# A recurrence kernel whose first, last and closing stages are rewritten: constants and loads set apart, last segment without lists for a next one, closing block in another order

## The chip, the cores and the metric

One core of a Trainium2 chip runs one program. The metric is the device time of that program in microseconds (us), the median of several executions. The engines are PE (TensorE), DVE (VectorE), ACT (ScalarE), POOL (GpSimd) and SP (SyncE, which only issues DMAs here). PEld is TensorE's weight load.

## The reference

The program computes four layers in a row: a gated delta-rule attention, a small mixture of experts, a softmax attention and a second mixture of experts, each with a residual and a layer norm. The change touches the first alone. Input x is (2, 1024, 128), with 8 heads, keys of 64 and values of 128 channels:

```
q, k, v = silu(conv4(x @ Wq.T)), silu(conv4(x @ Wk.T)) * 64**-0.5, silu(conv4(x @ Wv.T))
a    = sigmoid(x @ Wa.T + ba)          # decay, one number per value channel
beta = sigmoid(x @ Wb.T + bb)          # one number per head
for t in range(T):                     # S is (batch, head, 64, 128), from zero
    err = k_t @ S - v_t
    S   = a_t * S - beta_t * outer(k_t, err)
    o_t = q_t @ S
o = (o - mean) * rsqrt(var + 1e-5) * ln_w + ln_b
return (o * sigmoid(x @ Wg.T)) @ Wo.T
```

## The kernel before, in words

`delta_attention` is four blocks. A block ends when every engine has come to its end and met the others at a barrier, so it lasts as long as its slowest engine or load.

**First block (L176 to L213).** SP issues all loads: Wq, Wk, Wv into `wraw`, four copies of the convolution taps into `wtap` (1 MB each), small ones, `wo`, the input `xT`, `wa`, `wg`, `conv_b`, `ln_w`, `ln_b` and the residual `x_tok`. It waits for the last eight of them. DVE clears `state`, `kq` and `mt` (L201 to L203), multiplies weights and taps in four operations (L207) and scales small tensors and `wo` (L213). POOL builds the constants (`make_constants`, L76 to L127): the identity, a centring matrix, the head masks that the recurrence multiplies with, and masks that only later layers use.

**Second block (L634 to L686).** It prepares segment 0 (64 time steps of both batches): PE makes the projections with their convolution (L345), ACT their activations, POOL products of neighbouring keys (`near`, L538), then 16 copies of keys and queries into `kq` (L552), then scaled values (L527). DVE computes decays and their prefix products (`scan`, L560) and the inverses of small triangular blocks (L482 to L504), and last applies the head masks to the first products (`dve_masks`, L582).

**The recurrence (L696 to L920).** There are 16 segments of 4 chunks of 16 steps, two batches, so 8 "halves" in a segment. A half starts chunk `cc` of batch `x` and ends the previous chunk of the other batch `y`. Inside a chunk four sub-blocks are solved one after another: DVE multiplies and reduces (`solve`, L873 and L876), PE transposes the result (`turn`, L726), ACT copies it (`keep`, L830), PE takes its share off the rest (`take_off`, L737). Then `finish` (L743, L750) and DVE's `update` of the state (L889) let `start` (L708, L715) begin the next chunk of that batch. Every engine's order is written out by hand. Between these steps stand the items of a ring of three PSUM banks, from a list with four slots for each half:

```python
BOTH = [["k0.0"], ["k0.1"], ["k1.0"], ["k1.1", "p0"],
        ["q0.0"], ["q0.1"], ["b", "a0"], ["n", "a1", "p1"],
        ["wo.0"], ["wo.1"], ["a2"], ["a3", "p2"],
        ["g0.0"], ["g0.1"], ["c0"], ["p3"],
        ["g1.0"], ["g1.1"], ["c1"], ["p4"],
        ["var", "q1.0"], ["q1.1"], ["v0.0"], ["v0.1", "p5"],
        ["v1.0"], ["v1.1"], ["v2.0"], ["v2.1", "p6"],
        ["v3.0"], ["v3.1"], ["dt"], ["p7"]]
```

`k`, `q`, `v`, `a`, `b`, `n` and `dt` prepare the next segment, `p` are key products for the coming chunk, and `wo`, `g`, `c` and `var` finish the outputs of the segment before (projection with `wo`, gate, centred values, variance). The last segment runs the same list, so it prepares a segment that is not used. DVE's parts of this work are cut into pieces as well (`dve_piece`, L419).

**Closing block (L922 to L950).** It finishes the outputs of segment 14 first (normalised, gated, projected, L426 to L437), then makes gate, centred values and variance of segment 15. Its reciprocal standard deviation is spread to all partitions by way of DRAM and POOL (L613 to L619, L567, L568), then come normalising, gating and projecting again.

## Time and profile before

| | us |
|---|---|
| median of 3 runs (1963.08 to 1965.64) | 1964.63 |
| the profiled execution, its own time | 1965.2 |
| its span in the trace | 1963.5 |
| first block, to 32.6 | 32.6 |
| second block, 32.6 to 79.5 | 46.9 |
| recurrence, segments 0 to 14, to 999.6 | 920.1 |
| recurrence, segment 15, to 1060.7, and its last steps to 1069.3 | 69.7 |
| closing block, to 1101.8 | 32.5 |
| the other three layers | 861.7 |
| first block: POOL's last constant ends; the last load, `x_tok`, lands | 32.1; 27.2 |
| second block: DVE's chain without a pause, from L484 to L582 | 53.9 to 77.2 |
| segment 15, fourth and fifth half, from `start` to `start` | 6.3; 6.9 |
| closing block: the deviations have landed, L426 begins | 1092.9 |

Over the span PE is busy 87%, DVE 72%, ACT 51% and POOL 31%. The stages follow each other with a barrier between, so a stage's share of the time is read from that stage alone.

### The profile page before, as it was taken

The numbers are of one execution on the slowest core, as the hardware profiler recorded it, in microseconds if no ns is written. First come the engines' busy times: TensorE is split into PE (matmuls) and PEld (weight loads), VectorE is DVE, ScalarE is ACT, GpSimd is POOL, SyncE is SP. The second block draws the span as 40 slices with busy tenths as digits, with TensorE's granted clock in tenths as the row PEclk, the third lists the DMA queues.
The fourth block names the chain that finished last, engine by engine and source line by source line (L and its number), as shares of the span: only waits on it lengthen the run. The fifth ranks groups of instructions, "written<-read, shape, count | busy, mean of one in ns | idle before, by whom it ended". The sixth has DMA issues, their size and how long they took to land. (4 is left out here: it accounts for less than half of the span.)

```text
span 1963.5 us, 42737 instructions
## 1 busy us (share of the span) xinstructions
PE 1717.9 (87%) x15860; PEld 1464.6 (75%) x15860; DVE 1410.0 (72%) x3247; ACT 998.0 (51%) x2633; POOL 611.8 (31%) x986
## 2 busy tenths in 40 slices
PE   3599999899999999999997299799999999998795
PEld 2488788787878778778786266588888888888795
DVE  4687777877778777787776477566666666664777
ACT  1356555455555555556553222555666665653353
POOL 6254345443455434554344000000000000001653
PEclk9799999999999999999998699899999999999898
DMA  4123331223313333222330200890000000003232
GB/s 187 52 73 69 74 81 47 68 69 76 75 46 72 73 74 66 56 72 72 75 73 24 87 1 0 138 58 1 2 2 1 2 1 2 1 2 103 66 89 75
DMA packets 151328, 108.18 MB, mean 55 GB/s; under 512 B 34220, under 2 KB 139384, under 8 KB 150232
## 3 DMA queue, kind: packets, MB, share of 16 engines
q1 hardware_dynamic: 148632, 100.36, 23.3%
q0 software_dynamic: 2496, 5.13, 0.8%
q8 instruction: 127, 2.08, 0.5%
q14 instruction: 73, 0.60, 0.1%
HBM read 87.37 MB, written 18.09 MB: 54 GB/s over the span
## 5 line engine op out<-in xcount | busy, mean ns | idle before, releaser
L577 POOL TENSOR_TENSOR kfull<-kt,pair_rows 128x512 f32<-128x512 f32 x128 | 143.7, 1122 | 514.3 <-ACT kt L365 504.4
L345 PE MATMUL ps<-xT,taps 128*128 128x128 f32 x2176 | 294.0, 278 | 0.1
L345 PEld LDWEIGHTS ps<-xT,taps 128*128 128x128 f32 x2176 | 274.8, 196 | 8.0 <-issue 7.6
L830 ACT COPY wt<-ps 32x128 f32<-32x128 f32 x512 | 131.2, 256 | 260.8 <-PE ps L726 253.8
L1560 DVE TENSOR_REDUCE b_nmax<-ps 128x1 f32<-128x128 f32 (+7 forms) x256 | 180.6, 752 | 72.9 <-PE ps L1397 72.9
L873 DVE TENSOR_TENSOR prod<-ps,mt 128x128 f32<-128x128 f32 x512 | 147.4, 288 | 74.6 <-PE ps L737 59.0
L726 PE MATMUL ps<-ident,w 128*128 128x128 f32 x512 | 162.5, 317 | 34.1 <-ACT wt L830 19.7
L1537 POOL COPY b_spread<-b_inv 128x256 f32<-128x256 f32 x64 | 25.6, 401 | 513.0 <-DVE b_inv L1563 513.0
L876 DVE TENSOR_REDUCE w<-prod 128x32 f32<-128x128 f32 x512 | 146.6, 286 | 17.5
L726 PEld LDWEIGHTS ps<-ident,w 128*128 128x128 f32 x512 | 87.9, 172 | 84.6 <-DVE w L876 73.6
L1489 ACT ACTIVATE b_prob_long<-ps,b_nmax 128x1024 f32<-128x1024 f32 (+3 forms) x128 | 121.3, 952 | 55.8 <-DVE b_nmax L1560 55.8
L1397 PE MATMUL ps<-b_kT,b_qT 64*128 64x256 f32 (+1 forms) x1280 | 142.2, 366 | 0.0
L1429 PEld LDWEIGHTS ps<-b_probT,b_v 128*64 128x64 f32 x2304 | 124.5, 137 | 21.6 <-issue 20.8
L1429 PE MATMUL ps<-b_probT,b_v 128*64 128x128 f32 x2304 | 139.9, 276 | 0.6 <-ACT b_probT L1516 0.6
L737 PE MATMUL ps<-gq,wt 128*128 128x32 f32 x768 | 126.7, 247 | 11.3 <-ACT wt L830 10.1
L750 PE MATMUL ps<-wt,kfull 128*128 128x128 f32 x1024 | 136.2, 277 | 0.0
L737 PEld LDWEIGHTS ps<-gq,wt 128*128 128x128 f32 x768 | 116.7, 192 | 23.5 <-ACT wt L830 20.6
L560 POOL TENSOR_TENSOR di<-di 128x128 f32<-128x128 f32 x240 | 126.8, 528 | 17.6
L1570 DVE COPY b_probT<-ps 128x512 f32<-128x512 f32 (+1 forms) x192 | 115.4, 621 | 17.1 <-PE ps L1409 14.4
L1489 ACT ACTIVATE b_prob_short<-ps,b_nmax 128x128 f32<-128x128 f32 (+3 forms) x128 | 66.3, 522 | 118.0 <-DVE b_nmax L1560 118.0
L750 PEld LDWEIGHTS ps<-wt,kfull 128*128 128x128 f32 x1024 | 125.5, 193 | 0.0
L1397 PEld LDWEIGHTS ps<-b_kT,b_qT 64*128 64x128 f32 x1280 | 108.1, 187 | 13.8
(281 smaller groups left out, 3888.7 us busy)
## 6 DMA issues: line engine op xcount, KB each, us to landing
decay<-ends_dram SPq DMA_DIRECT2D x256, 128.0 KB, 5.8
gn<-near_dram SPq DMA_DIRECT2D x34, 384.0 KB, 6.6
slots_dram<-zero SPq DMA_DIRECT2D x1, 9216.0 KB, 58.8
rr<-rates_dram SPq DMA_DIRECT2D x34, 256.0 KB, 4.4
sq<-rstd_dram SPq DMA_DIRECT2D x17, 512.0 KB, 3.6
wtap<-in_taps SPq DMA_DIRECT2D x4, 1024.0 KB, 11.3
f_w<-in_f_w SPq DMA_DIRECT2D x2, 2048.0 KB, 11.0
s_xb<-slots_dram SPq DMA_DIRECT2D x46, 64.5 KB, 1.9
```

Of the source, the lines that this page charges most:

```text
L345: mm = pe.matmul(part, lhsT=taps[:, tap, t * P:(t + 1) * P], rhs=xT[:, :, columns(at_next) - LOOK + tap:columns(at_next) - LOOK + tap + TS ...
L577: nc.gpsimd.tensor_tensor(kfull[:, n % 4, :, :], kt[:, n % 2, :].unsqueeze(1).to_broadcast([P, G, P]), cst["pair_rows"][:, :].unsqueeze(2) ...
L726: pe.transpose(ps[:, 2, 0:P], w[:, b, :, :, :].rearrange("p i h s -> p (i h s)"), cst["ident"][:, :]).then_inc(wt_ready[b], 1)
L737: pe.matmul(ps[:, b, cols], lhsT=wt[:, b, :], rhs=gq[:, n % 4, 0, cols], start=False, stop=True, skip_group_check=True).then_inc(z_ready[b ...
L750: mm = pe.matmul(ps[:, 4 + b, g * P:(g + 1) * P], lhsT=kfull[:, n % 4, g, :], rhs=wt[:, b, :], start=False, stop=True, skip_group_check=True)
L830: nc.scalar.copy(wt[rows, b, :], ps[rows, 2, 0:P]).then_inc(wt_kept[b], 1)
L873: ch.step(nc.vector.tensor_tensor(prod[:, b, :, :, :], zi, mtc[:, :, b, NB * c + i, :, :], ALU.mult))
L876: nc.vector.tensor_reduce(w[:, b, i, :, :], prod[:, b, :, :, :], axis=AX.X, op=ALU.add).then_inc(w_ready[b], 1)
L1397: mm = pe.matmul(scores_of(w, long, h)[:, c0:c1], lhsT=qT[rows, f, b * T + i * P:b * T + (i + 1) * P], rhs=kT[rows, f, b * T + c0:b * T + ...
L1429: pe.matmul(ps[cols, 7, long * P:(long + 1) * P], lhsT=v[:, f, b * TT + j, cols], rhs=probT[:, at_probT(w, long, h * n + j), :], start=(j ...
L1489: nc.scalar.activation(prob[long][:, h, 0:tiles(w, long) * P], scores_of(w, long, h), ACT.Exp, bias=nmax[:, w % 2, j:j + 1], accum_out=tot ...
L1560: nc.vector.tensor_reduce(nmax[:, w % 2, j:j + 1], scores_of(w, j // 2, j % 2), axis=AX.X, op=ALU.max, negate=True).then_inc(max_done, 1)
```

## The change

- `make_constants` keeps what the first block and PE's first work need. The rest becomes `make_masks`, which POOL runs in the second block, between `near` and the 16 copies; DVE waits for it (`masks_made`) only before its last step there.
- The fill of `mt` with zeros moves from DVE to POOL in the first block.
- Loads of `wo`, `wg` and `x_tok` go to the end of SP's order. The first block waits for none of them: DVE waits for `wo` at the head of the second block and scales it there, SP waits for `wg` and `x_tok` at that block's end.
- In segment 15 the lists hold only `wo`, `g`, `c`, `var` and `p0` to `p6`; the DVE, ACT, POOL and SP work for a next segment is left out there as well.
- The closing block is written anew. PE takes the centred values of segment 15 first, then the gate, then the variance; segment 14's outputs are finished while the standard deviation of segment 15 travels. Segment 15 has buffers of its own (`cs_last`, `sq_last`, `gate_last`, in the room of `taps`).

```diff
-    def __init__(self, slots, by_vector):
+    def __init__(self, slots, by_vector, ending=None):
+        self.slots, self.by_vector, self.ending = slots, by_vector, ending or slots
...
+    def slots_of(self, f):
+        return self.ending if f == NS - 1 else self.slots
...
-    ch.step(nc.gpsimd.memset(cst["mean_col"][:, :], 1.0 / P))
...
+def make_masks(nc, ch, cst):
+    select = nc.gpsimd.affine_select
     ch.step(nc.gpsimd.memset(cst["head_masks"][:, :, :], -1.0 / DK))
...
-                                     (bias_b[:, 0:1], d["bb"]), (wo[:, :, :], d["WoT"])):
+                                     (bias_b[:, 0:1], d["bb"])):
                         sp.dma_start(dst, src).then_inc(load_b, 16)
...
-                    for dst, src in ((wa[:, :], d["WaT"]), (wg[:, :], d["WgT"]), (conv_b[:, :], d["conv_b"]),
-                                     (ln_w[:, :], d["ln_w"]), (ln_b[:, :], d["ln_b"]), (res[:, 1:, :], d["x_tok"])):
+                    for dst, src in ((wa[:, :], d["WaT"]), (conv_b[:, :], d["conv_b"]),
+                                     (ln_w[:, :], d["ln_w"]), (ln_b[:, :], d["ln_b"])):
                         sp.dma_start(dst, src).then_inc(load_w, 16)
-                    sp.wait_ge(load_w, 16 * 8)
+                    sp.dma_start(wo[:, :, :], d["WoT"]).then_inc(load_wo, 16)
+                    for dst, src in ((wg[:, :], d["WgT"]), (res[:, 1:, :], d["x_tok"])):
+                        sp.dma_start(dst, src).then_inc(load_late, 16)
+                    sp.wait_ge(load_w, 16 * 6)
...
                     make_constants(nc, pool, cst_made, cst)
+                    nc.gpsimd.memset(mt[:, :, :, :, :], 0.0)
...
-                    nc.vector.memset(mt[:, :, :, :, :], 0.0)
...
-        both = Ring(BOTH, BY_DVE)
+        both = Ring(BOTH, BY_DVE, [[x for x in part if x.split(".")[0] in POST + PRODUCTS[:-1]] for part in BOTH])
...
+                sp.wait_ge(load_late, 16 * 2)
...
                 pool_prepare(pool, only_pre, 0, 0, "near")
+                make_masks(nc, Chain(pool, S["masks_chain"]), cst)
+                nc.gpsimd.memset(cst["mean_col"][:, :], 1.0 / P).then_inc(S["masks_made"], 1)
                 pool_prepare(pool, only_pre, 0, 0, 0)
...
+                dve.wait_ge(load_wo, 16)
+                nc.vector.tensor_scalar(wo[:, :, :], wo[:, :, :], 0.5, None, ALU.mult)
...
                 dve.wait_ge(z_ready[0], 1)
+                dve.wait_ge(S["masks_made"], 1)
                 dve_masks(0, first_products, w_ready[0])
...
-                    if c == 1:
+                    if c == 1 and f < NS - 1:
                         sp_spread_rates(sp, both, f, 1 - f % 2)
...
-                    if j == 5:
+                    if j == 5 and f < NS - 1:
                         scan(ch, nc.gpsimd.tensor_tensor, f, nx)
...
+        cs_last, sq_last, gate_last = (taps[:, k, 0:H * N] for k in range(3))
...
+                for k in range(2):
+                    pe.matmul(ps[:, k, :], lhsT=cst["centre"][:, :], rhs=of[:, k * HALF:(k + 1) * HALF], start=True,
+                              stop=True).then_inc(E["centred"], 1)
...
+                pe.wait_ge(E["squared"], 2)
...
+                mm.then_inc(E["var_done"], 1)
+                out(0, cs)
+                out(1, cs_last)
...
+                    act.wait_ge(E["centred"], k + 1)
+                    nc.scalar.activation(sq_last[:, part], ps[:, k, :], ACT.Square).then_inc(E["squared"], 1)
+                    nc.scalar.copy(cs_last[:, part], ps[:, k, :])
+                act.wait_ge(E["var_done"], 1)
+                nc.scalar.copy(var_rows[:, :], ps[:, 4, 0:PART]).then_inc(E["var_kept"], 1)
+                norm(0, cs[:, :])
...
+                scale(cs, sq)
+                gating(0, cs, gate)
+                add(0)
+                dve.wait_ge(S["rstd_in"], 16)
+                scale(cs_last, sq_last)
+                dve.wait_ge(E["gate_kept"], 2)
+                gating(1, cs_last, gate_last)
+                add(1)
```

How the instructions stand now. **POOL, second block.** The engine's order before, from `near` to the scaled values:

```order
L538 TENSOR_TENSOR near<-qk 128x128
L552 COPY kq<-qk 64x8x4x4 [waits a_near_done,a_ring_act]
L552 COPY kq<-qk 64x8x4x4 x7
L552 COPY kq<-qk 64x8x4x4 [waits a_near_done,a_ring_act,a_copied]
L552 COPY kq<-qk 64x8x4x4 x7
L527 TENSOR_TENSOR vd<-vd,di 128x32x15 [waits a_d_done,a_ring_act,a_copied]
```

and of the change the place where the masks come in (L113, L115 and L122 are the selects that were L98, L100 and L107), with the engine's end of them:

```order
L554 TENSOR_TENSOR near<-qk 128x128
L108 MEMSET head_masks 128x256
L113 AFFINE_SELECT head_masks<-head_masks 32x128 [waits a_masks_chain]
L115 AFFINE_SELECT head_masks<-head_masks 32x128 [waits a_masks_chain]
L118 MEMSET head_masks 32x32 [waits a_masks_chain]
...
L140 MEMSET ident 128x128 [waits a_masks_chain]
L141 AFFINE_SELECT ident<-ident 128x128 [waits a_masks_chain]
L689 MEMSET mean_col 128x1 [waits a_masks_chain]
L568 COPY kq<-qk 64x8x4x4 [waits a_near_done,a_ring_act]
L568 COPY kq<-qk 64x8x4x4 x7
```

Between `near` and the copies there are now 31 selects and 13 fills.

**PE, segment 15, the half with j = 6.** Before, from `start` to the end of the half:

```order
L715 MATMUL ps<-kq,state 64x8x8 x7
L726 MATMUL ps<-ident,w 128x128 [waits a_wt_kept1,a_w_ready1]
L345 MATMUL ps<-xT,taps 128x128 [waits a_ring_act]
L345 MATMUL ps<-xT,taps 128x128 x3
L737 MATMUL ps<-gq,wt 128x32 [waits a_wt_kept1]
L726 MATMUL ps<-ident,w 128x128 [waits a_wt_kept1,a_w_ready0]
L345 MATMUL ps<-xT,taps 128x128 x4
L737 MATMUL ps<-gq,wt 128x32 [waits a_ring_dve,a_wt_kept0]
L726 MATMUL ps<-ident,w 128x128 [waits a_wt_kept0,a_w_ready1]
```

and of the change the same stretch (L748 is `turn`, L759 `take_off`):

```order
L737 MATMUL ps<-kq,state 64x8x8 x7
L748 MATMUL ps<-ident,w 128x128 [waits a_wt_kept1,a_w_ready1]
L759 MATMUL ps<-gq,wt 128x32 [waits a_wt_kept1]
L748 MATMUL ps<-ident,w 128x128 [waits a_wt_kept1,a_w_ready0]
L759 MATMUL ps<-gq,wt 128x32 [waits a_ring_dve,a_wt_kept0]
L748 MATMUL ps<-ident,w 128x128 [waits a_wt_kept0,a_w_ready1]
```

The convolutions between the steps of the two chains are gone; what stands in the row now waits for ACT or DVE at each instruction.

**PE, closing block.** Before:

```order
L316 MATMUL ps<-wo,cs 128x128 [waits a_gated]
L316 MATMUL ps<-wo,cs 128x128 x3
L324 MATMUL ps<-xT,wg 128x128 x8
L328 MATMUL ps<-vd,centre 128x512 [waits a_ring_dve]
L328 MATMUL ps<-vd,centre 128x512 [waits a_ring_act]
L304 MATMUL ps<-sq,mean_rows 32x256 [waits a_ring_act]
```

and of the change:

```order
L961 MATMUL ps<-vd,centre 128x512 x2
L965 MATMUL ps<-xT,wg 128x128 x8
L971 MATMUL ps<-taps,mean_rows 32x256 [waits a_end_squared]
L971 MATMUL ps<-taps,mean_rows 32x256 x3
L955 MATMUL ps<-wo,cs 128x128 [waits a_end_gated]
```

The projection of segment 14 stood ahead of centring and variance, and stands behind them now.

## Rows read from the trace of the kernel before

**Rows 1.** Busy time by stage: window, length, each engine's busy time, PEclk, DMA share, GB/s
```profile
0.00:32.60 32.60, 0.00 (x0) 0.00 (x0) 21.20 (x11) 0.00 (x0) 27.94 (x60) 1.00 0.72 274
32.60:79.50 46.90, 24.22 (x162) 20.16 (x162) 24.96 (x45) 16.04 (x41) 15.16 (x28) 0.79 0.11 31
999.60:1060.70 61.10, 56.16 (x527) 48.63 (x527) 48.48 (x123) 33.65 (x96) 28.40 (x46) 1.00 0.34 68
1069.30:1101.80 32.50, 11.40 (x60) 9.46 (x60) 5.75 (x10) 6.11 (x9) 1.90 (x2) 0.63 0.05 17
```

**Rows 2.** Timeline of the first block, POOL and DVE: start, length, engine, line, operation
```profile
7.94 6.88 DVE L203 MEMSET mt<- 128x8192 f32 x1 [1.66 <-issue]
10.81 6.26 POOL L107 TENSOR_SCALAR_AFFINE_SELECT head_masks<-head_masks 32x32 f32<-32x32 f32 x1
...
17.14 2.44 POOL L98 TENSOR_SCALAR_AFFINE_SELECT head_masks<-head_masks 32x128 f32<-32x128 f32 x1
...
26.36 0.55 POOL L98 TENSOR_SCALAR_AFFINE_SELECT head_masks<-head_masks 32x128 f32<-32x128 f32 x1
```

**Rows 3.** Loads of the first block: tile wtap, SP's timeline, and time to landing
```profile
L207 DVE TENSOR_TENSOR taps<-wraw,wtap x4: 2228/2374/2459, 14.7 to 21.5; 128x2048 f32<-128x2048 f32 x4
DMA to landing us min/median/max: 8.3/11.3/14.4
2.19 2.31 SPq L182 DMA_DIRECT2D wtap<-in_taps  x4
14.91 0.45 SPq L190 DMA_DIRECT2D ln_b<-in_ln_b  x1
ln_b<-in_ln_b SPq DMA_DIRECT2D x1, 0.5 KB, 10.3
```

**Rows 4.** Timeline of the second block, POOL and DVE
```profile
34.02 0.95 POOL L667 MEMSET cs<- 128x1024 f32 x1
...
41.96 1.78 POOL L538 TENSOR_TENSOR near<-qk 128x384 f32<-128x384 f32 x3 [5.20 <-ACT qk L405]
...
51.85 5.42 POOL L552 COPY kq<-qk 64x128 f32<-64x128 f32 x16 [8.11 <-ACT qk L403]
...
66.34 1.49 DVE L492 TENSOR_TENSOR tmp<-gn,mt 128x256 f32<-128x256 f32 x1
...
72.33 0.62 DVE L492 TENSOR_TENSOR tmp<-gn,mt 128x256 f32<-128x256 f32 x1
```

**Rows 5.** Timeline of segment 15 and of its last steps, the solve chain
```profile
1004.73 0.30 PE L726 MATMUL ps<-ident,w 128*128 128x128 f32 x1
...
1005.09 1.06 PE L750 MATMUL ps<-wt,kfull 128*128 128x128 f32 x8
...
1006.19 0.69 DVE L889 TENSOR_TENSOR state<-ps,decay 128x512 f32<-128x512 f32 x1 [0.60 <-PE ps L750]
...
1029.79 0.69 DVE L889 TENSOR_TENSOR state<-ps,decay 128x512 f32<-128x512 f32 x1
...
1031.26 0.29 DVE L873 TENSOR_TENSOR prod<-ps,mt 128x128 f32<-128x128 f32 x1
...
1061.65 0.28 DVE L873 TENSOR_TENSOR prod<-ps,mt 128x128 f32<-128x128 f32 x1
...
1062.31 0.33 PE L726 MATMUL ps<-ident,w 128*128 128x128 f32 x1 [2.11 <-DVE w L876]
...
1063.65 0.29 DVE L873 TENSOR_TENSOR prod<-ps,mt 128x128 f32<-128x128 f32 x1 [1.40 <-PE ps L737]
```

**Rows 6.** Busy time in a stretch at the end of the recurrence, columns as in rows 1
```profile
1059.00:1062.00 3.00, 1.20 (x9) 0.83 (x8) 2.93 (x6) 0.76 (x2) 0.80 (x1) 1.00 0.00 0
```

**Rows 7.** Timeline of the closing block
```profile
1076.67 1.95 PE L324 MATMUL ps<-xT,wg 128*128 128x128 f32 x16
...
1078.46 1.88 PE L328 MATMUL ps<-vd,centre 128*128 128x512 f32 x4
...
1082.43 0.37 ACT L372 COPY var_rows<-ps 128x256 f32<-128x256 f32 x1 [0.84 <-PE ps L304]
```

More of the change, by code:

```diff
@@ L855, in _ @@
                         act_norm(act, both, f)
-                    if j in (3, 4):
+                    if j in (3, 4) and f < NS - 1:
                         act_diagonal(act, f, 1 - f % 2, j - 3)
@@ L925, in _, with out @@
             def _(pe):
-                for item in only_post.names:
-                    pe_item(pe, only_post, 0, 1, item, 0, NS - 1)
-                for item in only_post.slots[0]:
-                    pe_item(pe, only_post, 1, 1, item, 0, NS - 1)
+                def out(k, values):
+                    pe.wait_ge(E["gated"], 2 * k + 2)
+                    for h in range(H):
+                        mm = pe.matmul(ps[:, 6 + k, 0:C], lhsT=values[:, h * N:(h + 1) * N], rhs=wo[:, h, :], start=(h == 0),
+                                       stop=(h == H - 1))
+                    mm.then_inc(E["out_done"], 1)
@@ L931, in _ @@
+                pe.wait_ge(E["squared"], 2)
+                for u in range(4):
+                    mm = pe.matmul(ps[32 * u:32 * u + 32, 4, 0:PART], lhsT=cst["mean_rows"][:, :],
+                                   rhs=sq_last[:, u * PART:(u + 1) * PART], start=True, stop=True, skip_group_check=True)
+                mm.then_inc(E["var_done"], 1)
+                out(0, cs)
+                out(1, cs_last)
             @block.scalar
             def _(act):
-                act_norm(act, only_post, 0)
@@ L934, in _, with norm @@
-                for item in only_post.order:
-                    act_item(act, only_post, 0, 1, item)
-                act_norm(act, only_post, 1)
+                def norm(k, values):
+                    act.wait_ge(E["scaled"], 2 * k + 2)
+                    nc.scalar.activation(values, values, ACT.Identity, bias=ln_b[:, 0:1], scale=ln_w[:, 0:1]).then_inc(
+                        E["normed"], 1)
+                for k in range(2):
+                    part = slice(k * HALF, (k + 1) * HALF)
+                    act.wait_ge(E["centred"], k + 1)
+                    nc.scalar.activation(sq_last[:, part], ps[:, k, :], ACT.Square).then_inc(E["squared"], 1)
+                    nc.scalar.copy(cs_last[:, part], ps[:, k, :])
@@ L938, in _ @@
+                act.wait_ge(E["var_done"], 1)
+                nc.scalar.copy(var_rows[:, :], ps[:, 4, 0:PART]).then_inc(E["var_kept"], 1)
+                norm(0, cs[:, :])
+                for k in range(2):
+                    act.wait_ge(E["gate_done"], k + 1)
+                    nc.scalar.activation(gate_last[:, k * HALF:(k + 1) * HALF], ps[:, 2 + k, :], ACT.Tanh, scale=0.5).then_inc(
+                        E["gate_kept"], 1)
+                norm(1, cs_last)
             @block.gpsimd
@@ L953, in delta_attention, with scale, gating @@
-        stage_end(nc, every)
+                def scale(values, factors):
+                    for k in range(2):
+                        part = slice(k * HALF, (k + 1) * HALF)
+                        nc.vector.tensor_tensor(values[:, part], values[:, part], factors[:, part], ALU.mult).then_inc(
+                            E["scaled"], 1)
+                def gating(n, values, gates):
+                    dve.wait_ge(E["normed"], n + 1)
+                    for k in range(2):
+                        part = slice(k * HALF, (k + 1) * HALF)
+                        stt(out=values[:, part], in0=gates[:, part], scalar=1.0, in1=values[:, part], op0=ALU.add,
+                            op1=ALU.mult).then_inc(E["gated"], 1)
@@ L956, in layer_norm @@
+                add(1)
+        stage_end(nc, every + list(E.values()))
 def layer_norm(nc, ctx, cst, ps, res, xT, name, loads=(), arrived=(), out=None):
```

66 lines of the change are left out of this document (45 added, 21 removed).

## The prediction

> **What bounds the kernel now.** I read the table of windows by stage first, since barriers part the stages, and then the timeline of each stage that the change touches, asking what ends last there.
>
> The first block lasts 32.6 us. DVE is busy for 21.2 of them, POOL for 27.9 [rows 1]. POOL ends last: its list of constants reaches to 32.1, and the last load to be waited for lands before 28. That list is stretched by DVE. A select takes 0.55 us alone, 2.44 beside DVE's products of weights and taps, and a smaller one took 6.26 [rows 2].
>
> The second block, 46.9 us, has no busy engine [rows 1]. DVE's chain ends it: from 53.9 to 77.2 it stands still nowhere, while POOL waits.
>
> Segment 15 takes 61.1 us with PE busy for 56.2 [rows 1]. PE is the bound there, and much of its work prepares a segment that does not exist.
>
> The closing block takes 32.5 us with PE busy for 11.4 [rows 1]: one serial path, in which the variance of segment 15 is copied out only at 1082.4 [rows 7], 13.1 us in; the way from there to the block's end, DMAs by DRAM and then norm, gate and projection, is 19.4.
>
> **First block.** Removed from POOL: 31 selects and 13 small fills. Added: the fill of `mt`, 8192 elements. A fill of 1024 takes 0.95 us there [rows 4], so 8 x 0.95 = 7.6, from 3.4 to 11. DVE loses its own fill, 6.88 us [rows 2], and is free at 6.3. Its four products, 2.2 to 2.5 us each, began at 14.7 behind that fill. The taps land 8.3 to 14.4 us after issues that begin at 2.2 and end at 4.5 [rows 3], so from 10.5 to about 18; the last product then ends at 20.3, the small scalings at 20.7. The loads decide: `ln_b`, issued at 14.91, landed 10.3 later, at 25.2 [rows 3]. Two loads of 512 KB, `wo` and `wg`, now stand behind it. Three MB of taps land within 7.5 us (10.5 to 18), so 512 KB are 1.25 us: `ln_b` lands at 22.7. Before, the next block began 0.5 us behind POOL's end, so now it begins at 23.1 in place of 32.6: **-9.5**. Bounds: -6.9 if `ln_b` lands no earlier (25.2 + 0.5), -11.4 if DVE were the last (20.7 + 0.5).
>
> `wo` lands about 1.3 us after `ln_b`. DVE waits for it at the head of the second block and scales it in some 0.7 us, and has nothing to do until 15 us into that block: 0. `x_tok` lands by 28, while SP's first own DMA of the block comes 11 us in: 0. Without that cover each would cost its own time.
>
> **Second block.** `near` ends at 43.7 [rows 4], 11.1 us into the block. The masks come next: 16 large selects at 0.61 with the gap, 15 small ones at about 0.3, 13 fills at about 0.2 make 17 us. Alone they would end 28 us in; the copies (5.4 us for 16 [rows 4], begun 19 us in before) then end at 34. PE's first products were held until 33.4 by DVE's scan, and DVE took them only 44 us in: covered by 10 us. The price lies elsewhere: while masks and copies last, DVE's chain meets POOL. DVE's four products, with no gap between, took 2.23 us at the least and 2.46 at the most [rows 3], the longest ones those with a large select just ahead: 0.23 for 0.55 of POOL. The three POOL operations per DVE operation that I count let about 18 selects (4 large, 14 small) fall beside DVE's chain: 4 x 0.23 + 14 x 0.06 = 1.7, and the copies, nine more than now beside it, 0.5: **+2.2**. Bounds: 0 where DVE finds the gaps, and the whole POOL operation each time: 4 x 0.55 + 14 x 0.2 + 9 x 0.34 = 8.1. For the upper end speaks L492, 1.49 us beside a POOL product of two inputs and 0.62 without one [rows 4]; I stay near the lower value since these are selects and copies, of one input, as in the row of 2.46.
>
> The Trainium skill (SBUF — State Buffer, "SBUF: two separate sides") calls the port that DVE and GpSimd share "an exclusive lock, not a bandwidth split", held for the whole instruction. It speaks against this part of the change. By it the term would be the upper end, some 8 us; the trace agrees for L492 and shows less than half of it for the selects.
>
> **Segment 15.** Gone from PE are 16 tiles of convolution, `a`, `b`, `n`, `dt` and `p7`, from DVE the decays and inverses, from POOL `scan`, copies and scaled values. What is left is bounded by the chain of the two batches, so I add one half up from update to update. From L889 to the solve of the other batch, 1.47 (1029.79 to 1031.26); once around solve, turn, keep, take off, 2.00 (1061.65 to 1063.65); solve to turn 0.66 (to 1062.31); turn to L750 0.36 (1004.73 to 1005.09); L750 to L889 1.10 [rows 5]. The sum is 5.6. PE's own row (product of keys, then `start`) makes `start` 0.1 late: 5.7, times 8 is 45.6. On top: scaling, and ACT's norm of 1.24 us ahead of a `keep`, 0.5 in the first half and 1.2 in the second; the projection between the steps of the third, 0.8; gate and centring in the fourth and fifth, 0.5 together. That makes 48.6, and 61.1 - 48.6 = **-12.5**. Bounds: halves four and five, which carry only `g` and `c` already, take 6.3 and 6.9 now; eight of 6.6 would be 52.8, so -8.3. The path without any delay, 44.8, and half of the additions, 1.5, give -14.8. What is late next is DVE's solve, not a DMA: the decay rows for chunk 63 are asked for three chunks ahead.
>
> **Closing block.** PE begins with centring (1.88 us), gate (1.95) [rows 7] and variance (0.64). These rows were taken at 2.4 GHz. In this block the granted clock is 0.63 on average [rows 1]: it stood at 1.2 GHz from the recurrence's end through PE's idle start, and rose to 2.4 in the course of the first projection. With about 4 us of it at 1.2 GHz, the 4.5 us of work become 6.5, and the copy of the variance begins 6.7 us in, not 13.1: **-6.4**. Bounds: full clock 4.7 in (-8.4), 1.2 GHz throughout 9.2 in (-3.9). The outputs of segment 14 take 1.29 + 1.24 + 1.29 + 3.6 + 0.3 and lie inside the 10.5 us until the deviations land: 0. The way from the copy to the end keeps its 19.4.
>
> **Sum.** -9.5 + 2.2 - 12.5 - 6.4 = -26.2. From the profiled execution's 1965.2 that gives 1939.0. The median of the runs lies 0.6 below that execution, so I say **1938.5**. About 0.2% (3.9 us) can be told from no change.
>
> **Rivals.**
> - *The port is a full lock.* The second block pays 8.1 in place of 2.2, and the total is 1944.4. For it: L492, and the select of 2.44. Against: 2.46 beside 2.23. The page named above states this mechanism. Chance 0.16.
> - *The late loads do not get out of the way,* so the first block doesn't do what it says. All loads share the same DMA engines; if the small ones behind `wa` land at 25.2 as before, the first block gives 6.9: 1941.1. For it: SP's issues were held up at `ln_w`. Against: loads landed in the order of issue. Chance 0.12.
> - *The clock falls inside segment 15.* After a stretch in which PE was busy for 1.2 of 3 us [rows 6] the clock fell to 1.2 GHz. There it stays at full speed as long as convolutions fill the gaps. In the new halves PE works for some 3.5 of 5.7 us. If it fell, L750's 1.06 [rows 5] and the other passes would put 1.5 on each half, and projection and gate 1 more: 61, no gain, 1951. Against: PE still has work in every part of a half. Chance 0.08.
> - *Slower: POOL starves.* In the first block a select waited for a whole DVE operation, 2.4 us. If each of the 31 waited like that in the second block, masks would take 31 x 2.4 = 74, the block would end about 90 us in and not at 47: +43 on -28.4, hence 1979.5. It turns slower than before from 1.9 us a select on. Against: DVE's operations there are 0.4 to 0.8 us long. Chance 0.02.
>
> **How the numbers follow.** The forecast has 0.62: the likeliest, so 1938.5. Its own bounds run from 1931 (all gains near their ends) to 1945. The range 1932 to 1947 takes in the first two rivals and leaves out the clock (0.08), starving (0.02) and about 0.08 of tails. Faster by over 0.2%: all but starving and a heap of mishaps, 0.97; within it 0.01; slower 0.02.
>
> **What would show it.** The second block should begin near 23 with SP's load the last to be waited for and POOL idle from 11. Masks should stand between 11 and 32 us into the block, selects up to 1.1 us long, and DVE's chain end 2 us later than the 77.2 - 32.6 of now; if its operations beside selects last 0.5 us longer each, it is the lock. Segment 15's halves should be 5.6 to 6.9 us from L889 to L889, at PEclk 1.00. In the closing block the variance copy should begin 6 to 7 us in. I am wrong if a block's end is held by something I gave no price, if the halves stay above 6.3, or if the clock reads 0.50 within the segment.

## The result and the profile after

The change takes 1940.31 us, the median of 4 runs (1936.63 to 1940.86), against 1964.33 (1963.08 to 1965.64) for the kernel before. The ratio is 0.9874, with a 95% interval from 0.9857 to 0.9891, so the kernel is faster by some 24 us. The profiled execution took 1940.86 us, its span 1938.9. All times below are of executions in the chip's fast state; one in a slow state, of 4190.78 us in the run with the masks made twice, is left out.

By stage, from barrier to barrier (the second column is the length of the stage in the trace of before):

| stage | before | after | difference | forecast |
|---|---|---|---|---|
| first block | 32.6 | 23.15 | -9.5 | -9.5 |
| second block | 46.9 | 46.55 | -0.4 | +2.2 |
| segments 0 to 14 | 920.1 | 921.2 | +1.1 | 0 |
| segment 15 with the last steps | 69.7 | 60.9 | -8.8 | -12.5 |
| closing block | 32.5 | 25.3 | -7.2 | -6.4 |
| the other three layers | 861.7 | 861.75 | 0 | 0 |
| span | 1963.5 | 1938.9 | -24.6 | -26.2 |

Of the 1.1 us in segments 0 to 14, 1.0 lies in the very first half (9.1 us from `start` to `start`, 8.15 before). The traces show the clock there too: its second eight passes of convolution take 1.91 us (L361 at 73.54) and took 1.06 (L345 at 83.32), and the half reads 0.69 where it read 0.78.

A trace is one execution, and a stage that no edit touches differs between traces. In the nine traces below whose kernels leave the first block as in the change it lasts 22.3 to 22.9 us, and in the nine that leave the second block so, that one lasts 45.7 to 47.4.

These are the windows of after: three stages, segment 15 with its last steps, and under the dots its eight halves, from `start` to `start`, the last with the last steps. The columns are those of [rows 1]: length, then busy time of PE, PEld, DVE, ACT and POOL, PEclk, DMA share, GB/s.

```profile
0.00:23.15 23.15, 0.00 (x0) 0.00 (x0) 13.75 (x9) 0.00 (x1) 8.94 (x18) 1.00 0.90 344
23.15:69.70 46.55, 25.38 (x162) 21.06 (x163) 26.94 (x46) 16.14 (x41) 36.19 (x72) 0.77 0.19 52
990.91:1051.85 60.94, 49.01 (x384) 40.33 (x384) 33.81 (x102) 19.65 (x58) 10.42 (x10) 0.83 0.21 44
1051.85:1077.15 25.30, 12.22 (x60) 9.23 (x60) 5.75 (x10) 5.87 (x9) 1.91 (x2) 0.67 0.06 22
...
990.91:999.49 8.58, 6.80 (x42) 5.53 (x42) 5.95 (x17) 1.25 (x5) 1.28 (x1) 0.66 0.49 115
999.49:1007.70 8.21, 6.25 (x43) 5.29 (x42) 4.39 (x12) 2.95 (x7) 1.04 (x1) 0.73 0.27 73
1007.70:1013.93 6.23, 5.67 (x59) 5.19 (x58) 3.55 (x12) 1.79 (x6) 1.04 (x1) 1.00 0.31 42
1013.93:1019.67 5.74, 5.74 (x53) 4.72 (x52) 3.53 (x12) 3.47 (x9) 1.04 (x1) 1.00 0.37 44
1019.67:1025.41 5.74, 5.74 (x53) 4.72 (x52) 3.52 (x12) 3.47 (x9) 1.04 (x1) 1.00 0.02 5
1025.41:1031.23 5.82, 4.92 (x52) 3.71 (x51) 3.54 (x12) 2.16 (x7) 1.04 (x1) 1.00 0.02 3
1031.23:1038.37 7.14, 5.89 (x43) 5.01 (x42) 3.84 (x13) 1.78 (x6) 2.90 (x3) 0.76 0.02 3
1038.37:1051.85 13.48, 8.02 (x55) 6.16 (x53) 5.47 (x18) 2.78 (x9) 1.04 (x1) 0.74 0.13 40
```

Read the PEclk column first. Before it stood at 1.00 over the whole segment [rows 1]. Now the halves 3 to 6 read 1.00 and last 5.7 to 6.2 us, and the halves 1, 2 and 7 read 0.66, 0.73 and 0.76 and last 8.6, 8.2 and 7.1. That is where the missing part of the forecast is. The timeline of PE shows what it is made of, the product of the state (L750 before [rows 5]) in half 1 and in half 3:

```profile
996.28 1.91 PE L772 MATMUL ps<-wt,kfull 128*128 128x128 f32 x8
...
1012.27 1.06 PE L772 MATMUL ps<-wt,kfull 128*128 128x128 f32 x8
```

The same eight passes take 1.91 us at 1.2 GHz and 1.06 at 2.4. The fall itself comes in half 1, and this stretch stands at the lower level throughout:

```profile
993.60:1000.30 6.70, 5.84 (x27) 4.81 (x27) 3.60 (x11) 1.34 (x5) 0.23 (x1) 0.50 0.67 166
```

The first block of after, POOL and DVE, and below it the landing of `ln_b` (median us from issue; it was issued at 10.79):

```profile
3.30 6.93 POOL L217 MEMSET mt<- 128x8192 f32 x1
...
18.19 2.29 DVE L226 TENSOR_TENSOR taps<-wraw,wtap 128x2048 f32<-128x2048 f32 x1 [0.27 <-DMA wtap<-in_taps]
...
23.15 0.96 POOL L681 MEMSET vd<- 128x1024 f32 x1 [12.92 <-POOLq L192]
...
ln_b<-in_ln_b SPq DMA_DIRECT2D x1, 0.5 KB, 12.0
```

POOL ends at 10.2 and stands idle for 12.9 us; DVE ends at 20.7; `ln_b` lands at 22.8 and the next block begins at 23.15. POOL's list, which ended the block at 32.1, has gone from the path, and a load has taken its place.

The second block, POOL and DVE:

```profile
54.76 7.37 POOL L568 COPY kq<-qk 64x128 f32<-64x128 f32 x16
...
62.21 3.00 POOL L543 TENSOR_TENSOR vd<-vd,di 128x480 f32<-128x480 f32 x2
62.64 1.52 DVE L514 TENSOR_TENSOR tmp<-gn,mt 128x256 f32<-128x256 f32 x1
64.20 1.49 DVE L516 TENSOR_TENSOR tmp<-gn,mt 128x256 f32<-128x256 f32 x1
...
66.90 0.41 DVE L598 TENSOR_TENSOR gq<-ps,head_masks 128x256 f32<-128x256 f32 x1
```

The 16 copies stretch from 5.42 [rows 4] to 7.37 us, but DVE's chain, from its first L500 (43.52) to the end of its last L520 (66.99), lasts 23.5 us where it lasted 23.0. The chain is a steadier measure than the block: in the nine other traces it lasts 23.3 to 23.5 us. DVE reaches its last step 4.8 us behind the copies: masks and copies are hidden.

The closing block:

```profile
1051.85 3.54 PE L961 MATMUL ps<-vd,centre 128*128 128x512 f32 x4 [1.66 <-PEq L85]
...
1057.81 0.37 ACT L990 COPY var_rows<-ps 128x256 f32<-128x256 f32 x1 [1.31 <-PE ps L971]
...
1060.70 2.75 PE L955 MATMUL ps<-wo,cs 128*128 128x128 f32 x16 [2.96 <-DVE cs L1026]
...
1072.27 3.59 PE L955 MATMUL ps<-wo,taps 128*128 128x128 f32 x16 [8.82 <-DVE taps L1026]
```

The variance is copied 6.0 us in, not 13.1 [rows 7]. Centring takes 3.54 us where it took 1.88 [rows 7].

### The profile page after: what moved, and what is told of

It reads as the page before. It is cut to its first block and busy times, and to the rows that moved or that the text cites. A ratio compares the mean times of both kernels' runs of the same rounds, so it can differ in the third digit from the quotient of the medians.

```text
span 1938.9 us, 42270 instructions
## 1 busy us (share of the span) xinstructions
PE 1711.4 (88%) x15702; PEld 1455.7 (75%) x15702; DVE 1386.2 (71%) x3217; ACT 984.5 (51%) x2593; POOL 595.3 (31%) x951
## 3 DMA queue, kind: packets, MB, share of 16 engines
q8 instruction: 125, 2.05, 0.5%
## 5 line engine op out<-in xcount | busy, mean ns | idle before, releaser
L361 PE MATMUL ps<-xT,taps 128*128 128x128 f32 x2048 | 278.9, 279 | 0.1
L361 PEld LDWEIGHTS ps<-xT,taps 128*128 128x128 f32 x2048 | 260.6, 197 | 7.6 <-issue 7.2
L748 PE MATMUL ps<-ident,w 128*128 128x128 f32 x512 | 163.0, 318 | 34.7 <-ACT wt L853 18.5
L748 PEld LDWEIGHTS ps<-ident,w 128*128 128x128 f32 x512 | 87.9, 172 | 84.8 <-DVE w L899 73.6
L759 PE MATMUL ps<-gq,wt 128*128 128x32 f32 x768 | 128.3, 249 | 14.2 <-ACT wt L853 13.1
L1518 PEld LDWEIGHTS ps<-b_probT,b_v 128*64 128x64 f32 x2304 | 124.5, 137 | 21.7 <-issue 20.9
L759 PEld LDWEIGHTS ps<-gq,wt 128*128 128x128 f32 x768 | 117.7, 194 | 28.3 <-ACT wt L853 25.3
L576 POOL TENSOR_TENSOR di<-di 128x128 f32<-128x128 f32 x225 | 118.7, 527 | 16.5
## 6 DMA issues: line engine op xcount, KB each, us to landing
f_w<-in_f_w SPq DMA_DIRECT2D x2, 2048.0 KB, 10.7
```

Of the source, the lines that this page charges most:

```text
L361: mm = pe.matmul(part, lhsT=taps[:, tap, t * P:(t + 1) * P], rhs=xT[:, :, columns(at_next) - LOOK + tap:columns(at_next) - LOOK + tap + TS ...
L748: pe.transpose(ps[:, 2, 0:P], w[:, b, :, :, :].rearrange("p i h s -> p (i h s)"), cst["ident"][:, :]).then_inc(wt_ready[b], 1)
L759: pe.matmul(ps[:, b, cols], lhsT=wt[:, b, :], rhs=gq[:, n % 4, 0, cols], start=False, stop=True, skip_group_check=True).then_inc(z_ready[b ...
L1518: pe.matmul(ps[cols, 7, long * P:(long + 1) * P], lhsT=v[:, f, b * TT + j, cols], rhs=probT[:, at_probT(w, long, h * n + j), :], start=(j ...
```

## The experiments

**The parts, one undone at a time.** Four kernels, each the change with one part put back.

Masks to the first block, `mt` to DVE:

```diff
                     make_constants(nc, pool, cst_made, cst)
-                    nc.gpsimd.memset(mt[:, :, :, :, :], 0.0)
+                    make_masks(nc, Chain(pool, masks_chain), cst)
...
-                make_masks(nc, Chain(pool, S["masks_chain"]), cst)
```

> The changed kernel with one part undone: the masks are made by POOL in the first block again, and mt is filled by DVE again; loads, last segment and closing block stay changed. Theory (POOL's list ended the first block, and the masks cost DVE's chain in the second block 0.5 us): first block back to 32.6 us from 23.15, second block 46.0 in place of 46.5, total 1949.4. Rival (the shared port is held for whole instructions, and the second block is as long as it was only because something else got shorter by as much): without masks there the second block falls to 43 or less, total 1946. Rival (the loads end the first block, not POOL): first block stays at 23 to 24, total 1940.

Measured: 1948.85 us (1944.36 to 1953.61). The first block lasts 33.5 us, the second 46.25, and DVE's chain there 22.7. POOL ends the first block again:

```profile
33.09 0.10 POOL L218 MEMSET mean_col<- 128x1 f32 x1
33.49 0.95 POOL L683 MEMSET vd<- 128x1024 f32 x1 [0.30 <-POOLq L192]
```

The theory holds. Without the masks the second block is 0.3 us shorter, less than it differs between traces, and DVE's chain 0.8 (22.7 for 23.5).

Loads in their old order, all waited for in the first block:

```diff
-                                     (bias_b[:, 0:1], d["bb"])):
+                                     (bias_b[:, 0:1], d["bb"]), (wo[:, :, :], d["WoT"])):
...
-                    sp.wait_ge(load_w, 16 * 6)
+                    sp.wait_ge(load_w, 16 * 8)
```

> The changed kernel with one part undone: wo, wg and x_tok stand in the old places of SP's order and the first block waits for all of them; masks stay in the second block. Theory (the last load that is waited for ends the first block, and loads land in the order of issue): the block ends 0.5 us behind x_tok's landing, which was at 27.2 before, so 27.7 in place of 23.15: +4.5, total 1944.8, second block unchanged. Rival (order is of no weight, the small loads land when the taps are through): the block ends at 23 to 24, total 1940 to 1941.

Measured: 1946.67 us (1945.00 to 1947.69), first block 28.15 us (+5.0, forecast +4.5), second 46.7. The block now ends 0.4 us behind the landing of `x_tok` (27.7). So with the masks moved alone the block goes from 32.6 to 28.15 us, with the loads moved alone (the run above) it stays at 33.5; the -9.5 needs both.

Full lists in segment 15:

```diff
-        both = Ring(BOTH, BY_DVE, [[x for x in part if x.split(".")[0] in POST + PRODUCTS[:-1]] for part in BOTH])
+        both = Ring(BOTH, BY_DVE)
...
-                    if j == 5 and f < NS - 1:
+                    if j == 5:
```

> The changed kernel with one part undone: segment 15 runs the full lists for a next segment again, on all engines. Theory (what the short lists gained is the 8.8 us that the traces show, and half clock in three of the halves took the rest of the forecast 12.5): segment 15 with its last steps 69.7 us, granted clock 1.00 through all its halves, the 8 passes of the state product 1.06 us in every half, total 1949.1. Rival (the first two halves are long because of the scaling and normalising of DVE and ACT, not because of the clock): the first two halves are as long as now or longer, 8.6 and 8.2 or more, even though the clock is 1.00, and the total is the same 1949.

Measured: 1948.58 us (1948.36 to 1949.61), segment 15 with its last steps 69.5 us. The windows of its halves 1, 2 and 7:

```profile
991.99:1000.05 8.06, 7.48 (x73) 7.04 (x74) 6.11 (x17) 2.24 (x9) 1.29 (x1) 1.00 0.53 107
1000.05:1009.16 9.11, 8.00 (x77) 6.64 (x76) 4.80 (x13) 7.25 (x21) 2.79 (x4) 1.00 0.08 22
...
1038.14:1046.00 7.86, 7.65 (x75) 7.06 (x74) 6.93 (x16) 2.96 (x12) 7.48 (x17) 1.00 0.11 37
```

PE is busy for 7.5 of 8.1 us and the clock reads 1.00. With short lists it has less to do and the first half is longer, 8.58 us. The term is measured (8.6 us in the trace); whether the clock or DVE's scaling makes the first two halves long, this run can't tell, since PE's own work fills them here.

The old closing block:

```diff
-                def out(k, values):
-                    pe.wait_ge(E["gated"], 2 * k + 2)
...
+                for item in only_post.names:
+                    pe_item(pe, only_post, 0, 1, item, 0, NS - 1)
```

> The changed kernel with one part undone: the closing block in its old order. Theory: variance copied 13 us in and the block 32.5 us again, against 25.3: +7.2, total 1947.5. Rival (the block starts at 1.2 GHz in both orders, so the old order now suffers more, since PE's projection, gate and centring all stand ahead of the variance): variance copied 14 to 16 us in, block 34 to 35, total 1949 to 1950.

Measured: 1944.76 us (1942.56 to 1948.66), 2.7 less than forecast. The block itself costs more than forecast, 33.2 us with the variance copied 13.6 us in (+7.9). The stages that this edit leaves alone are shorter than in the change: the first two by 0.9 us together, segment 15 with its last steps by 1.2, and the three layers behind by 2.0 (859.7). The first 40 us of those layers in two windows of 20, here and below it in the change:

```profile
1082.67:1102.67 20.00, 8.49 (x48) 8.02 (x48) 12.22 (x25) 8.56 (x15) 0.00 (x0) 0.64 0.52 188
1102.67:1122.67 20.00, 12.00 (x46) 7.38 (x47) 14.57 (x32) 3.58 (x6) 0.00 (x0) 0.67 0.00 1
...
1077.15:1097.15 20.00, 9.62 (x44) 9.07 (x45) 11.43 (x24) 8.29 (x14) 0.00 (x0) 0.54 0.48 187
1097.15:1117.15 20.00, 10.87 (x39) 6.96 (x40) 13.06 (x26) 2.67 (x5) 0.00 (x0) 0.60 0.00 0
```

The clock is higher here. That is no price of the new order as such. The change and the runs with masks first, loads first, masks twice and small loads moved read 0.54 or 0.55 and then 0.60, and their last three layers take 861.7 to 862.6 us. The runs with full lists and with unread matmuls in the segment alone have the new order too, read 0.63 to 0.65 and 0.66 to 0.68, and take 859.0 to 859.7. The clock at the head of these layers isn't all of it, since the kernel before reads 0.63 and 0.68 and takes 861.6. So a total moves by 3 us and more with what happens behind the edit.

**Matmuls that nobody reads.** Is it the clock that makes the halves 1, 2 and 7 long? PE gets matmuls of 128x128 into the PSUM bank that the next item will overwrite, two behind each of the first three slots of the halves 1, 2, 7 and 8. They change no result.

```diff
+                def spin(j, k, count):
...
+                    for _ in range(count):
+                        pe.matmul(ps[:, BANKS[(r - 1) % len(BANKS)], 0:P], lhsT=cst["ident"][:, :], rhs=cst["centre"][:, :],
+                                  start=True, stop=True, skip_group_check=True)
...
+                        if f == NS - 1 and j in (0, 1, 6, 7) and k in (0, 1, 2):
+                            spin(j, k, 2)
```

> The changed kernel, and in segment 15 PE gets matmuls that nobody reads: two of 128x128 behind each of the first three slots of the halves 1, 2, 7 and 8 (24 matmuls, some 0.23 us each at full clock, 1.35 us in a half). Theory (the clock fell to 1.2 GHz in these halves because PE had too little to do, and that is why they last 8.6, 8.2 and 7.1 us and not 5.8): granted clock 0.9 to 1.00 there, halves 7.5, 6.6 and 6.0, last steps 0.5 shorter, the closing block's centring 1.9 in place of 3.5; together 4 to 6 us less than the change: 1935 to 1936. Rival (scaling, normalising and the tail of segment 14's vector work make these halves long): halves as long as now plus up to 1.35 us each, total 1940 to 1944.

Measured: 1935.05 us (1931.55 to 1935.89), ratio to the kernel before 0.9844 (0.9830 to 0.9857). Halves 1, 2, 3, 7, and 8 with the last steps:

```profile
989.79:996.52 6.73, 5.80 (x53) 5.03 (x54) 5.34 (x15) 1.24 (x5) 1.29 (x1) 1.00 0.46 107
996.52:1003.26 6.74, 5.64 (x55) 4.89 (x54) 4.64 (x14) 2.95 (x7) 1.04 (x1) 1.00 0.56 129
1003.26:1009.49 6.23, 5.67 (x59) 5.19 (x58) 3.73 (x13) 1.78 (x6) 1.04 (x1) 1.00 0.34 42
1026.80:1032.46 5.66, 5.54 (x55) 4.89 (x54) 3.52 (x12) 1.78 (x6) 2.90 (x3) 1.00 0.02 1
1032.46:1045.60 13.14, 8.80 (x66) 7.27 (x65) 5.71 (x18) 2.78 (x9) 1.04 (x1) 0.78 0.11 41
```

The halves fall from 8.58, 8.21 and 7.14 us to 6.73, 6.74 and 5.66 with more work on PE, and each reads 1.00. That is the clock, and it rules the rival out for what was lost: scaling and normalising are still there. The halves 1 and 2 stay 1.0 us above the 5.74 of halves 4 and 5; how much of that scaling and normalising make was not measured. Segment 15 with its last steps takes 55.8 us, 5.1 less than in the change. In the last steps the clock still falls, and centring begins the closing block at 1.2 GHz as before (3.75 us): that part of the expectation failed. The gate begins at 1.2 GHz as well (2.41 us, 1.95 in the change), so the closing block is 1.2 us longer, 26.5. The three layers behind are 2.7 shorter (859.0).

The dose doubled, `spin(j, k, 4)`:

> As the run before, with four such matmuls in place of two (2.7 us in a half at full clock). Theory: the clock is 1.00 as well, but the matmuls now stand in the way of the two solve chains: halves of 6.5 to 7, total between the dose of two and the change, 1936 to 1939. Rival (no clock effect): 1943 to 1948.

Measured: 1937.22 us (1936.74 to 1937.84). Halves 1, 2 and 7 read 1.00 and last 7.07, 6.90 and 6.34 us. The clock has nothing more to give, and the matmuls stand in the way.

The dose halved, `spin(j, k, 1)`:

> As the run with two unread matmuls a slot, with one (0.7 us in a half at full clock). Theory: what is bought is the clock alone, so if it reads 1.00 with the dose of one, the halves 1 and 2 last 6.4 to 6.7 and the total is that of dose two or up to 0.5 less, 1934 to 1935; if it falls in one of them, that half lasts 8 again and the total is 1936 to 1939. Rival (the unread matmuls help by something other than the clock, such as keeping the queue of PE fed): half of the gain of dose two, halves of 7.6, whatever the clock reads.

Measured: 1934.54 us (1932.62 to 1936.66). The halves 1 and 2 last as long as with dose two:

```profile
991.35:998.08 6.73, 5.33 (x47) 4.37 (x48) 5.35 (x15) 1.23 (x5) 1.29 (x1) 1.00 0.46 108
998.08:1004.82 6.74, 5.08 (x49) 4.22 (x48) 4.64 (x14) 2.95 (x7) 1.04 (x1) 1.00 0.55 128
```

What helps doesn't grow with the dose; it comes with the clock's 1.00. Twelve matmuls in the segment are enough.

**The port that DVE and POOL share.** The masks are made twice in the second block, so that selects stand beside all of DVE's chain.

```diff
-                make_masks(nc, Chain(pool, S["masks_chain"]), cst)
+                masks = Chain(pool, S["masks_chain"])
+                for _ in range(2):
+                    make_masks(nc, masks, cst)
```

> The changed kernel with the masks made twice in the second block, the same instructions once more behind the first, so that POOL's selects stand beside the whole of DVE's chain there (23.4 us long in the change, 22.9 in the kernel before). Theory (a select costs DVE a quarter of a microsecond at most, most find the gaps): DVE's chain 23.5 to 24.5 us. Rival (the port is held for whole instructions): another 16 selects beside the chain cost their own length, the chain lasts 28 us or more. In both cases POOL now ends the block: masks to 76, copies to 82, scaled values and keys to 85; second block 62 us in place of 46.5, total 1955 to 1957.

Measured: 1954.43 us, the median of three (1951.10 to 1956.55), second block 59.2 us. DVE's chain lasts 22.2 us, less than in the change. It must be compared like for like: here POOL's two scaled products come after the chain, while in the other kernels two of DVE's operations meet them and take 1.5 us in place of 0.62 and 0.60. Without that 1.8 the chain of the kernel with no masks there is 22.7 - 1.8 = 20.9. So 32 selects and their fills beside the whole chain cost DVE 1.3 us, where a DVE held off for each whole select would, by estimate, have lost over 10 (17 of them are large selects of 0.54 us, 9.2 us already). One of DVE's operations with a select beginning beside it:

```profile
62.86 0.63 DVE L514 TENSOR_TENSOR tmp<-gn,mt 128x256 f32<-128x256 f32 x1
63.02 0.86 POOL L113 TENSOR_SCALAR_AFFINE_SELECT head_masks<-head_masks 32x128 f32<-32x128 f32 x1
63.52 0.66 DVE L516 TENSOR_TENSOR tmp<-gn,mt 128x256 f32<-128x256 f32 x1
```

It is the select that gets longer (0.86 us, 0.54 alone). The same L514 took 1.52 us beside a POOL product of two inputs, above.

**Small loads.** If `ln_b` ends the first block, move it, and the next one is earlier.

```diff
+                    sp.dma_start(conv_b[:, :], d["conv_b"]).then_inc(load_w, 16)
...
+                    sp.dma_start(wa[:, :], d["WaT"]).then_inc(load_w, 16)
...
-                    for dst, src in ((wg[:, :], d["WgT"]), (res[:, 1:, :], d["x_tok"])):
+                    for dst, src in ((wg[:, :], d["WgT"]), (res[:, 1:, :], d["x_tok"]), (ln_w[:, :], d["ln_w"]),
+                                     (ln_b[:, :], d["ln_b"])):
```

> The changed kernel with three small loads moved: conv_b ahead of xT, ln_w and ln_b behind x_tok among those that the first block doesn't wait for. Theory (the last load that is waited for ends the block, 0.4 us behind its landing): the last is now wa, which landed at 20.7 and may land a little earlier; the block ends at 21.0 to 21.3 (DVE's last scaling ends at 20.7) in place of 23.15; total 1938.3. Rival (SP's own issuing of small loads holds the queue up, and what is moved forward delays the input behind it): block at 22 to 23, total 1939.5 to 1940.5.

Measured: 1941.04 us (1937.67 to 1943.56), first block 22.65 us, within the 22.3 to 22.9 of kernels that move nothing there. No gain: the rival was right. SP's issue of `wa` and of what follows, the landing of `wa`, and the next block's first operation:

```profile
9.14 0.44 SPq L205 DMA_DIRECT2D wa<-in_WaT  x1
9.62 1.21 SPq L206 DMA_DIRECT2D wo<-in_WoT  x1
10.87 2.11 SPq L209 DMA_DIRECT2D wg<-in_WgT  x1
13.02 2.11 SPq L209 DMA_DIRECT2D stream<-in_x_tok  x1
...
wa<-in_WaT SPq DMA_DIRECT2D x1, 512.0 KB, 13.1
...
22.65 0.96 POOL L681 MEMSET vd<- 128x1024 f32 x1 [12.43 <-POOLq L192]
```

`wa` lands at 22.2, 0.4 us ahead of the block's end. It was issued at 7.88 and landed at 20.7 in the change. The last load waited for does end the block; only it comes 1.6 us later itself, being issued 1.3 later.

**A version that beats both.** Matmuls that nobody reads to the end of the layer:

```diff
                 turn(last_chunk, 1, 2)
+                spin(7, 3, 2)
                 take_off(last_chunk, 1, 2)
+                spin(7, 3, 4)
...
+                spin_last(10)
                 out(0, cs)
+                spin_last(24)
                 out(1, cs_last)
```

> The kernel with two unread matmuls a slot, and more of them to the end: between the last steps of the recurrence (16), and in the closing block 10 ahead of segment 14's projection and 24 ahead of the last one, while PE waits there. Theory (half clock costs 0.9 us in the last steps, 2.3 in centring and gate, 1.7 in the last projection): last steps at 1.00, centring 1.9 us, variance copied 4.7 to 5.5 us into the block, last projection 1.9 in place of 3.6; half 8 with last steps 12 in place of 13.1, closing block 23 to 24 in place of 26.5; total 3 to 5 us less than with the dose of two alone, 1930 to 1932. Rival (the barrier's pause is enough for the clock to fall, and matmuls behind it don't bring it back in time): 1934 to 1937, the extra matmuls standing in the way.

Measured: 1932.15 us (1928.55 to 1934.97). The variance is copied 4.4 us into the block, centring takes 1.95. The five times spread over 6.4 us, and the trace is of the second fastest (1928.67). The extra matmuls behind segment 14's projection (x48 are 24 of them, two passes each), and the last projection:

```profile
1054.79 5.52 PE L976 MATMUL ps<-centre,ident 128*128 128x128 f32 x48
1065.47 3.78 PE L970 MATMUL ps<-wo,taps 128*128 128x128 f32 x16 [5.16 <-DVE taps L1048]
```

The 24 matmuls, at full clock, ended 5.2 us too early, and the projection ran at 1.2 GHz: this part of the expectation failed. The closing block takes 24.9 us. The next run changes three things against this one: 42 matmuls in place of the 24, two in place of the eight behind the last step, and no last update of the state, which nobody reads:

```diff
+                    if cc == last_chunk:
+                        return
                     if n >= 1:
                         pe.wait_ge(S["k_kept"], n)
...
-                spin(7, 3, 8)
+                spin(7, 3, 2)
...
-                spin_last(24)
+                spin_last(42)
```

> The kernel with unread matmuls to the end, with three things put right: 42 of them ahead of the last projection in place of 24 (the 24 ended 5.2 us before it, and it lasted 3.8 us at half clock), 2 in place of 8 behind the last step (the 8 ended 1.0 us behind DVE and held the barrier), and the last update of the state, which nobody reads, left out for both batches (the last product of the state with its DVE operation, and the decay rows for it). Theory: the last product and update no longer stand between the last outputs and the barrier, closing block begins 2.3 us sooner (half 8 with last steps 10.7 in place of 12.96); last projection 1.9 to 2.1 at full clock, closing block 23.1 in place of 24.9; total 4 us less than the run before, 1928. Rival (the barrier waits for something else, such as SP's DMAs, or the clock falls in the shorter tail): 1930 to 1932.

Measured: **1929.87 us** (1927.71 to 1930.68), ratio to the kernel before 0.9825 (0.9812 to 0.9839), against 0.9874 (0.9857 to 0.9891) for the change: 10 us faster than the change, by intervals that do not touch. Its gain over the run before, 2.3 us by the medians, is not clear of the spread (1928.55 to 1934.97 there). Half 8 with the last steps, the closing block, and the last projection:

```profile
1033.00:1042.77 9.77, 7.91 (x71) 6.71 (x69) 4.42 (x17) 2.78 (x9) 1.04 (x1) 1.00 0.16 56
1042.77:1065.43 22.66, 20.22 (x164) 18.16 (x164) 5.75 (x10) 5.78 (x9) 1.91 (x2) 1.00 0.08 24
...
1062.09 2.05 PE L975 MATMUL ps<-wo,taps 128*128 128x128 f32 x16 [0.61 <-DVE taps L1053]
```

Both stages are shorter than expected (10.7 and 23.1); the total is 1.9 us above the forecast 1928, since the layers behind take 860.5 us here and took 856.3 in the run before. At their head the clock reads 0.65 and 0.67 here and read 0.59 and 0.74; why they differ by that was not found.

The last update left out of the change, with no extra matmuls:

> The change as it is, with no unread matmuls, and only the last update of the state left out for both batches. Theory (the chain from the last solve to the barrier is shorter by the product, 1.9 at half clock, and the update): last steps 2.5 us shorter, total 1937.5 to 1938. Rival (with yet less work PE's clock stays down for longer, in half 8 and at the head of the closing block): part of it is given back, total 1939 to 1940.

Measured: 1937.93 us (1936.43 to 1940.34). The segment with its last steps takes 57.0 us, 4.0 less than in the change; 3.4 of that lie in half 8 with the last steps (10.06 us at PEclk 0.82, 13.48 at 0.74 before), 0.8 in half 1, in which the clock read 0.86 and not 0.66. No instruction is different up to there, so these 0.8 are the clock's own variation and no gain of the edit. The closing block is 0.8 longer (26.1) and reads 0.63 where the change read 0.67. So the closing block may give something back, as the rival said; the sum is where the theory put it.

## Why the prediction was right, and where not

The median came out at 1940.3 for 1938.5 foretold, inside the range. That it lies so near is partly luck: segment 15 gave 3.7 us less than its term and segments 0 to 14 took 1.1 more, while the second block came out 2.6 below its term and the closing block gave 0.8 more. Of the prediction's own signs of being wrong two came true, halves above 6.3 us (1, 2 and 7) and a clock of 0.50 within the segment. By steps:

- **First block, -9.5: right, and right in what ends the block.** `ln_b` was to land at 22.7 and the next block to begin at 23.1; they did so at 22.8 and 23.15. Undoing either part shows that POOL's list (33.5) and `x_tok` (28.15) had both to go. The rival of late loads that do not get out of the way is ruled out for `ln_b`, which landed at 25.2 before. Why it lands sooner is less sure than the sum has it: the sum counts the megabyte no longer ahead of it, but `ln_b` was also issued 4.1 us sooner (10.79 for 14.91), and with the small loads moved `wa` landed 1.6 us later when issued 1.3 later, with hardly more ahead of it. No run parts the two for `ln_b`. Nor does the first decimal mean much, since other traces of the same block give 22.3 to 22.9 us.
- **Second block, +2.2: mis-sized.** DVE's chain grew by 0.5 us, and the block got 0.4 shorter, since the chain begins 0.9 earlier in it (a difference of the size that untouched blocks show). The price of a select for DVE was taken from one row (0.23 us); the run with masks made twice gives 1.3 us for 32 of them, 0.04 each. The rival, a port held for the whole instruction, priced the term at 8.1 us from rows. The prediction named the rule of the Trainium skill for it (SBUF — State Buffer, "SBUF: two separate sides"), by which whichever of the two engines starts first holds the shared port for its whole instruction. The run with twice the masks speaks against it for selects; L514 and L516, at 1.5 us beside a POOL product of two inputs, agree with it. POOL did not starve either: no select took over 0.95 us.
- **Segment 15, -12.5: the step that failed.** The sum of a half (5.7 us) was right: the undisturbed halves last 5.74. What was wrong is that the term priced every half at 2.4 GHz. Three of eight read 0.66 to 0.76, and the term came to 8.8. The rival "the clock falls inside segment 15" had the mechanism but not the extent: it was priced for all eight halves (no gain), and in the change it struck three that have no projection, gate or centring in PE's list. Which ones is not fixed by the list: with the loads first the halves 1, 2 and 3 read 0.63, 0.70 and 0.87 (8.8, 8.6 and 7.0 us) and half 7 read 1.00 (5.7 us), and half 8 was spared in the change up to the last steps. "PE still has work in every part of a half" did not hold the clock; a single matmul more in a slot does. With the clock held in the halves the segment with its last steps takes 55.8 us, so the term would have been -13.9.
- **Closing block, -6.4: right, 0.8 too small.** The variance was copied 6.0 us in, 6.7 foretold. Centring ran at 1.2 GHz for its length, as assumed, and the clock was up again for the gate (1.95 us).
- **Hidden terms, all at 0:** `wo` is scaled at 23.64 in 1.02 us, and DVE has nothing else to do for 12 us; segment 14's projection ends at 1063.5, 4.8 us before the deviations land. `x_tok` landed at 27.3 and held nothing up. Segments 0 to 14 were put at 0 and took 1.1 more, 1.0 of it in the first half, by the clock.

## What to carry to other kernels

When a change takes filler work from PE and leaves a chain of small dependent steps, price the chain at both clocks, half by half, and read the granted clock before anything else in the new trace. If it reads below 1.00, try a few matmuls that nobody reads before rewriting the order; place them so that the last ends right before the work that counts. Where two things end a block together, here POOL's list and a load behind it, moving one gives only the gap between them. Before a total is read for one stage, compare the stages that the edit leaves alone: here they moved it by 3 us and more.

## What was not expected of the hardware

- The granted clock fell to 1.2 GHz inside a stretch in which PE was busy for 6.8 of 8.6 and 6.3 of 8.2 us by the trace (halves 1 and 2; part of that busy time is itself the slow clock), and read 1.00 with one more 128x128 matmul, some 0.25 us, behind each of three slots in a half.
- The same instructions read differently with what ran before them: the first 40 us of the three layers behind read 0.54 and 0.60 in the change and 0.63 and 0.68 with two unread matmuls a slot in the segment.
- After 5.2 us without work PE's last projection ran at 1.2 GHz (3.78 us); after 0.6 us it ran at 2.4 (2.05 us).
- POOL's selects and DVE's chain, mostly products of two inputs, share time almost freely (32 selects cost DVE 1.3 us; a select of 0.54 us took up to 0.95), while a POOL product of two inputs costs a DVE operation beside it 0.9 us.
- SP's issue of a load took 1.9 to 2.1 us for neighbouring loads at about 9 to 15 us, whatever they were: `ln_w`, `ln_b` and `wo` in the change, `wg`, `conv_b` and `ln_w` with the old order, and two in a row, `wg` and `x_tok`, with the small loads moved. In these three orders the loads that were issued so are among the 15th to the 17th load issued, so it goes with the place in the order, or with the time, and not with the load (single ones of them took 1.1 us, `conv_b`, and 3.2, `ln_w`, in the kernel before). A load of half a KB is no cheaper to issue there than one of a MB. Why was not found.
